# Ten one-column degree products: from a block of their own to single places between the matmuls of a block product

## The reference

```python
xn = _layernorm(x)
# GCNConv with self loops
deg = segment_sum(ones, dst)                 # edges into each node, and the self loop
dinv = where(deg > 0, rsqrt(deg), 0)
h = xn @ W                                   # 1250x1024 times 1024x1024
out = relu(segment_sum(h[src] * (dinv[src] * dinv[dst])[:, None], dst) + b)
# beside it: attention without softmax (relu(q) relu(k)^T v), then x = x + out + attn @ Wo + bo
# then a feed-forward part with fake-quantized activations and weights
```

## Time and profile before

| | |
|---|---|
| time, median of 3 runs | 727.1 us (725.97 to 727.27) |
| the profiled execution's own time | 727.32 us |
| its span in the profile | 725.2 us |
| TensorE busy | 704.7 us (97% of the span) |
| VectorE busy | 550.3 us (76%) |
| GpSimd busy | 348.0 us (48%) |
| ScalarE busy | 232.5 us (32%) |
| mean granted clock of TensorE | 0.995 |

### The profile page before, as it was taken

The page is one execution under the profiler, slowest core; times in us unless marked ns, Lnnn a source line. Parts: engine busy times, 40 slices in busy tenths (PEclk is TensorE's granted clock), DMA queues, the critical chain, the costliest instruction groups (busy, mean ns, idle before and its releaser), DMA issues.

```text
span 725.2 us, 11607 instructions
## 1 busy us (share of the span) xinstructions
PE 704.7 (97%) x3801; PEld 362.7 (50%) x3801; DVE 550.3 (76%) x1036; ACT 232.5 (32%) x382; POOL 348.0 (48%) x441
## 2 busy tenths in 40 slices
PE   4999999999999999999999999999999999999996
PEld 2455555545555554566654444444444444446752
DVE  6878887888666778876697865869877779765766
ACT  5232334553333346554223334430100000013441
POOL 4566766899666778874354540011111111113317
PEclk9999999999999999999999999999999999999999
DMA  9652412464000000000000005153322122100607
GB/s 342 221 133 78 94 45 65 154 241 153 0 0 0 1 2 1 0 1 1 1 1 0 1 1 176 56 174 66 105 75 57 56 73 61 34 12 1 117 1 282
DMA packets 52803, 52.27 MB, mean 72 GB/s; under 512 B 36514, under 2 KB 37546, under 8 KB 52752
## 3 DMA queue, kind: packets, MB, share of 16 engines
q1 hardware_dynamic: 52752, 51.61, 24.2%
HBM read 37.96 MB, written 5.12 MB: 59 GB/s over the span
## 4 chain that ended last, share of the span: by engine, by line
PE 80%; DVE 10%; issue 4%; ACT 2%; DVEq 1%; POOL 1%; DMA 1%; POOLq 0%; SPq 0%
PE bank L625 18%; PE bank L862 14%; PE bank L699 12%; PE bank L735 12%; PE bank L806 12%; PE bank L910 3%; PE bank L610 2%; DVE mem L1464 2%; DVE mem L1238 2%; PE bank L939 2%; PE bank L642 2%; DVE counts L1352 2%; PE bank L798 1%; ACT mem L967 1%; DMA mem<-in_x 1%
## 5 line engine op out<-in xcount | busy, mean ns | idle before, releaser
L625 PE MATMUL bank<-mem 128*128 128x512 f16 x960 | 223.6, 382 | 3.3 <-ACT mem L967 1.8
L490 POOL TENSOR_SCALAR hot_src<-iota_p,src_col 125x128 bf16<-125x128 bf16 x252 | 186.0, 754 | 14.1 <-issue 14.1
L625 PEld LDWEIGHTS bank<-mem 128*128 128x128 f16 (+1 forms) x960 | 90.9, 98 | 100.1 <-issue 4.5
L1352 DVE TENSOR_TENSOR counts<-bank,counts 128x120 f32 x328 | 91.9, 280 | 41.8 <-PE bank L610 6.6
L862 PE MATMUL bank<-mem 128*128 128x512 f16 (+1 forms) x504 | 105.5, 369 | 0.0
L699 PE MATMUL bank<-mem 128*128 128x512 f16 (+2 forms) x576 | 105.1, 339 | 0.0
L735 PE MATMUL bank<-mem 128*128 128x512 f16 x420 | 92.8, 384 | 0.0
L806 PE MATMUL bank<-mem 128*128 128x512 f16 x400 | 88.0, 379 | 0.1
L862 PEld LDWEIGHTS bank<-mem 128*128 128x128 f16 x504 | 49.3, 98 | 53.7 <-issue 0.3
L699 PEld LDWEIGHTS bank<-mem 128*128 128x128 f16 (+1 forms) x576 | 55.3, 98 | 41.3
L569 POOL TENSOR_TENSOR cols<-cols 128x1 f32<-128x1 f32 x10 | 5.6, 555 | 139.1 <-DVE cols L1674 139.1
(11 more groups left out here) (176 smaller groups left out, 829.6 us busy)
## 6 DMA issues: line engine op xcount, KB each, us to landing
mem<-in_x SPq DMA_DIRECT2D x18, 512.0 KB, 3.9
out_x<-mem SPq DMA_DIRECT2D x9, 512.0 KB
mem<-in_L_mix_Wk SPq DMA_DIRECT2D x4, 1024.0 KB, 9.6
mem<-in_L_mix_Wv SPq DMA_DIRECT2D x4, 1024.0 KB, 8.7
mem<-in_L_mix_Wq SPq DMA_DIRECT2D x4, 1024.0 KB, 5.1
mem<-in_L_gnn_W SPq DMA_DIRECT2D x4, 1024.0 KB, 7.8
mem<-in_L_mix_Wo SPq DMA_DIRECT2D x4, 1024.0 KB, 6.5
mem<-in_L_ffn_w_down SPq DMA_DIRECT2D x4, 352.0 KB, 3.1
```

Source lines behind the costliest of these rows:

```text
L490: pool.tensor_scalar(hot_src[0:EC, i, c, :], iota_p[0:EC, :], src_col[0:EC, i, c:c + 1], None, ALU.is_equal).then_inc(S["hot_src_ready"], 1)
L625: last = pe.matmul(o[:, :], xT[:, a * K + k, bass.ds(t * P, P)], w16[i][:, k, b, :], start=(at == 0), stop=(at == len(parts) - 1))
L1352: dve.tensor_tensor(window, agg[i][:, k * WC:(k + 1) * WC], window, ALU.add).then_inc(S["adj_added"], 1)
```

## The change

The ten degree products leave their block. `product` gets a parameter `degrees`; for product 3 of pair 0 it is ten, and one degree product is issued ahead of each of the first ten of its 12 matmuls. The last of the ten still posts `SM["deg_full"]`. The wait for `SM["sources"]` stays where it was, and the waits of product 3 now stand ahead of the degree products too.

```diff
+            def degree(n):
+                return pe.matmul(agg[0][:, n:n + 1], sources[:, n * P:(n + 1) * P], ones, start=True, stop=True,
+                                 skip_group_check=True)
+
-            def product(j, left, right, o, fresh):
+            def product(j, left, right, o, fresh, degrees=0):
 
                 for k in range(K // 2):
-                    for a, b in ((0, 0), (0, 1), (1, 0)):
+                    for pass_n, (a, b) in enumerate(((0, 0), (0, 1), (1, 0))):
+                        n = 3 * k + pass_n
+                        if n < degrees:
+                            counted = degree(n)
+                            if n == degrees - 1:
+                                counted.then_inc(SM["deg_full"], 1)
...
                 if j == 0:
                     pe.wait_ge(SM["sources"], 1)
-                    for n in range(T):
-                        last = pe.matmul(agg[0][:, n:n + 1], sources[:, n * P:(n + 1) * P], ones, start=True, stop=True,
-                                         skip_group_check=True)
-                    last.then_inc(SM["deg_full"], 1)
-
-                if j == 0:
                     pe.wait_ge(S["q_lo"], 3 * K + 1)
...
                 pe.wait_ge(SG["s_lo"], 4 * j + 2)
-                product(j, 2, "T2", b1, True)
+                product(j, 2, "T2", b1, True, T if j == 0 else 0)
```

## The result

The changed kernel takes 730.11 us (median of 22 runs, 726.52 to 731.94), the kernel before 726.83 us (22 runs, 725.12 to 728.37). The ratio is 1.0035, with a 95% interval of 1.0025 to 1.0045. That is 1.8 to 3.3 us more. (The ratio lies near that of the means, 729.4 to 726.7; the medians are 3.3 us apart, because the times form groups.) The prediction said 728.0, with a range from 726.2 to 729.3, and most of its chance on no measurable difference.

The account below looks back on a forecast made before the run. TensorE was taken to bound the kernel, busy 704.7 of 725.2 us. Earlier start -0.15, nine degree products +1.28 and clock -0.2 sum to +0.9 us, so the median goes from 727.1 to 728.0 us, range 726.2 to 729.3.

Parts of the forecast that it names:

- rival 1: Degree products in product 3: no load hidden, or the fp16 load slow too; 0.22 us each, +1.85, 729.0 us; chance 0.21.
- these terms: TensorE at product 3 of pair 0: earlier start -0.15 us, nine degree products between matmuls +1.28 us at 0.14 each.
- the term of the clock: Around product 3: one 3.41 us half-speed stretch stays, losing 1.5 us over interleaved matmuls instead of 1.7: -0.2 us.
- the unit of the low level: In product 3 at half clock: one 512-column matmul, 0.427 us, plus a degree product, 0.14 if its loads aren't slowed.
- Rival 3: TensorE around product 3: low-clock stretch comes where it was absent, or a second one; +2.6 us, 729.7 us; chance 0.10.
- Rival 2: TensorE around product 3: clock stays at its upper level as one-column passes are spread; -0.6 us, 726.5 us; chance 0.16.

Follow-up runs that it names:

- e1: The changed kernel again without any edit, five more runs and another profile: 730.33 us, ratio 1.0046 to the kernel before.
- e7: The changed kernel with the ten degree products as a block again, but behind product 3's waits: 731.07 us, ratio 1.0059 to the kernel before.
- e3: The changed kernel with the ten degree products between the matmuls of product 4 instead of product 3: 728.24 us, ratio 1.0010 to the kernel before.
- e5: The kernel before, block in its old place, with VectorE's sum s4 moved behind the sources' post and the low halves: 726.85 us, ratio 0.9999.
- e4: The changed kernel with VectorE's sum s4 moved behind the sources' post and the low halves: 726.16 us, ratio 0.9988 to the kernel before.
- e10: The changed kernel with five unused wide matmuls behind product 2, filling half of the wait: 726.77 us, ratio 1.0004 to the kernel before.
- e2: The changed kernel with ten unused wide matmuls behind product 2, filling the wait: 727.19 us, ratio 1.000 to the kernel before.
- e9: The changed kernel with ten unused wide matmuls in the wait and the degree products as a block behind it: 727.38 us, ratio 1.0016.
- e8: The changed kernel with a degree product at every second matmul of products 3 and 4: 728.52 us, ratio 1.0025 to the kernel before.

## Why the prediction was wrong

**What held.** The block was cover for the wait on the low half of sum 2, and the edit turned it into idle time: 2.15 us, predicted 2.2. A degree product between two matmuls costs 0.138, predicted 0.14, one load hidden and one not. By rival 1's rule from the Trainium skill, page "TensorE: Matmul & The Clock Gate", section "Part 3: Packing small matmuls — row/col tiling", no load would be hidden; the trace of the changed kernel disagrees, with a load that starts with the matmul at 371.88. Nothing behind the degrees came later, in e1 neither: VectorE waits 0.79 us for them there, and GpSimd takes them up 15.3 us behind the start of product 1 as in the kernel before. At the upper clock the edit costs what these terms give: +1.13 us predicted, +0.9 by the medians of the lower groups (726.91 less 725.98).

**The step that failed** is the term of the clock, "against the 1.7 of before: -0.2 us". In its place the trace of e1 shows +1.6: 3.3 us lost against the 1.7 of before. (From upper group to upper group the result has 3.1 us more, of which 0.9 are the other terms; no run shows what the last 0.6 are.) The term was wrong twice. First, it took the low stretch to be as long after as before, 3.41 us, and priced it at 1.5. In the upper group it is twice as long (6.8 us in e1) and costs 3.3. The working did put degree loads that may slow down into the unit of the low level (it measured 0.67, the predicted ends were 0.57 and 0.71), but it did not ask whether a stretch with so little streaming in it would be the last. In e1 and e7 it is not; in e3, e5 and the kernel before, where the low stretch is dense, it is.

Second, the term took the low stretch for certain in the kernel before, from the one execution that was profiled. The groups suggest that it is missing in eight of 22 executions. The 80 runs of the kernel before beside the experiments say the same more clearly: 28 take up to 726.20 us, 26 of them with a mean granted clock of 0.999 or 1.000, and 52 take 726.69 or more, with 0.994 to 0.998. The medians of these groups are 1.6 to 1.7 us apart on each of the three chips, which is what the low stretch costs. No execution of the lower group of this kernel was profiled, so this is argued from size and clock and not seen. The edit makes the fall neither new nor certain. What it does show is more falls that last longer. With the wait shortened to 0.8 or 1.1 us or filled (e4, e10, e2), the thin stream had no upper group in 34 runs. With 2.15 us idle it had one in 15 of 22 and 5 of 5, and with 2.15 us idle and the block behind them five of the six runs of e7 are at 730.55 or more.

**Which rival.** Rival 3, a low stretch oftener or a second one, at 0.10 and 729.7 us. Its second form is what happens. It priced the step from one low stretch to two at 2.6 us in all; from upper group to upper group it is 3.1 in the result and 2.8 beside e1 (730.33 less 727.57). Rival 2 (the clock stays up, 726.5) describes the other third of the executions to 0.4 us. The median of a kernel with two groups follows the larger one, and my range ended at 729.3, under rival 3's 729.7. The Trainium skill, page "TensorE: Matmul & The Clock Gate", section "HAM oscillation — how this bites in real kernels", blames waits between bursts. e2 and e3 agree with it, with a wait of 2.15 us. I had given that too little weight against the one pattern that the trace of before showed.

**Left open.** Why a second low stretch follows in e1 and e7: the stream during the first, and the length without wide matmuls ahead of it, were not tested apart. Whether the thin stream also makes a first fall more likely: 20 of 27 runs with it and 7 of 12 in e3 don't tell. Why e9's block, behind wide matmuls, let the clock fall in two of 12 runs at most, while the kernel before, whose 0.4 us of idle time stands ahead of the same block, has 14 of 22 in its upper group; and whether the three times near 730 of e8 had two low stretches.

## What to carry to other kernels

Before small work is moved out of a block into a stream, look for the wait that the block hides; here the wait stayed and its cover went. The order that paid was the reverse: first make the awaited operand earlier (VectorE's order), then put as many small products in the rest of the wait as fit, and only the others into the stream. Where TensorE's clock is in play, one profile is one draw: ask for the spread of the times, and look at what TensorE does in and just after a wait, since a fall there lasted twice as long with a thin stream behind it (e1) as with a dense one (e3).

## What was not expected of the hardware

- A second low stretch followed the first where TensorE streamed little in the first: 6.8 us low with 0.43 us of streaming in each 0.67 (e1), or with one-column passes (e7), against 3.41 us with dense matmuls (e3, e5). That the thin streaming is the cause is argued from these five profiles.
- The hidden-and-unhidden pair of f32 loads costs more at the low level: a degree product between two matmuls takes 0.138 us at the upper level and 0.24 at the lower (e1).
- 2.2 us of extra wide matmuls in a wait made the kernel 3.1 us faster than the changed kernel beside it (e2 against e1).
